# Reordering the start of a gated attention and mixture-of-experts layer: weight loads on two queues, a weight product in split parts, statistics of six tiles first

## Time and profile before

| | |
|---|---|
| median of 3 runs | 493.73 us |
| the profiled execution | 495.23 us |
| its span, first to last instruction | 493.5 us |
| TensorE busy (2146 matmul records) | 477.6 us, 97% |
| VectorE, ScalarE, GpSimd busy | 64%, 42%, 42% |
| mean rate of the 16 DMA engines | 235 GB/s |
| granted clock of TensorE | 1.00 in every slice |

### The profile page before, as it was taken

One profiled execution on the slowest core, in us unless ns is written; L12 is line 12 of the kernel. 1 busy time (PEld: TensorE's weight loads), 2 busy tenths in 40 slices (PEclk: granted clock), 3 DMA queues, 4 the chain that ended last, 5 costly groups with the idle time before them and its releaser, 6 DMA issues.

```text
span 493.5 us, 7143 instructions
## 1 busy us (share of the span) xinstructions
PE 477.6 (97%) x2146; PEld 388.1 (79%) x2147; DVE 315.2 (64%) x474; ACT 207.7 (42%) x300; POOL 205.3 (42%) x288
## 2 busy tenths in 40 slices
PE   3999999999999999999999999999999999999995
PEld 1678696888888878877888888888888878888884
DVE  2656253479553435969888888863597754857762
ACT  1156274132531144836444444322665441544550
POOL 3035301003887849802100000645657874377134
PEclk9999999999999999999999999999999999999999
DMA  7862999965889699896899566888455864445512
GB/s 253 313 242 107 379 383 362 394 239 185 301 267 308 233 317 289 256 293 202 245 279 229 191 184 205 277 308 304 129 156 166 277 182 155 146 147 181 170 43 86
DMA packets 77694, 115.77 MB, mean 235 GB/s; under 512 B 6608, under 2 KB 36320, under 8 KB 77664
## 3 DMA queue, kind: packets, MB, share of 16 engines
q1 hardware_dynamic: 64448, 78.66, 50.6%
q0 software_dynamic: 7360, 25.19, 14.6%
q10 hardware_dynamic: 5856, 11.54, 6.8%
HBM read 66.09 MB, written 49.28 MB: 234 GB/s over the span
## 4 chain that ended last, share of the span: by engine, by line
PE 70%; POOL 10%; DVE 6%; DMA 6%; issue 5%; ACT 1%; SPq 1%; DVEq 0%; ACTq 0%; POOLq 0%
PE ab L1583 17%; PE ab L1584 17%; PE ab L1585 17%; POOL rows_scratch L759 6%; PE sc L1583 4%; PE sc L1585 4%; PE sc L1584 4%; PE sc L1599 3%; POOL W L748 3%; DMA xg<-rows_scratch 2%; PE tp L1633 2%; PE tp L1589 2%; DMA rows_scratch<-xb,pos 2%; DMA raw_o<-in_w_out_t 1%; DVE y L1462 1%
## 5 line engine op out<-in xcount | busy, mean ns | idle before, releaser
L776 POOL DMA_INDIRECT y<-y_scratch,pos x32 | 33.4, 1043 | 88.7 <-DMA y_scratch<-yt_so 74.1
L1583 PE MATMUL ab<-W,st_h 128*128 x156 | 60.8, 390 | 1.1 <-DVE st_l L1291 1.1
L1584 PE MATMUL ab<-W,st_h 128*128 x156 | 60.7, 389 | 0.0
L1585 PE MATMUL ab<-W,st_l 128*128 x156 | 60.7, 389 | 0.0
L759 POOL DMA_INDIRECT rows_scratch<-xb,pos x32 | 31.2, 976 | 50.9 <-DVEq L1279 42.7
L1583 PE MATMUL sc<-xt_h,t_h 128*128 128x512 f32 x128 | 50.1, 391 | 0.0
L1585 PE MATMUL sc<-xt_h,t_l 128*128 128x512 f32 x128 | 49.8, 389 | 0.0
L1584 PE MATMUL sc<-xt_l,t_h 128*128 128x512 f32 x128 | 49.8, 389 | 0.0
L1020 ACT CAST st_h<-tp 128x512 fp32r<-128x512 f32 x39 | 22.9, 587 | 41.1 <-PE ab L1585 40.2
L1583 PEld LDWEIGHTS ab<-W,st_h 128*128 128x128 f32 x156 | 29.3, 188 | 7.6 <-issue 1.5
L1347 DVE TENSOR_REDUCE small<-sc 128x1 f32<-128x1024 f32 x16 | 19.5, 1222 | 23.7 <-PE sc L1585 23.4
(11 more groups left out here) (269 smaller groups left out, 1199.1 us busy)
## 6 DMA issues: line engine op xcount, KB each, us to landing
rows_scratch<-xn ACTq DMA_DIRECT2D x3, 3328.0 KB, 19.3
xb<-in_expert_w POOLq DMA_DIRECT2D x6, 1024.0 KB, 9.1
xn<-rows_scratch SPq DMA_DIRECT2D x48, 128.0 KB, 3.4
xg<-rows_scratch SPq DMA_DIRECT2D x44, 128.0 KB, 3.0
y_scratch<-yt_own SPq DMA_DIRECT2D x20, 256.0 KB, 3.2
y_scratch<-yt_so SPq DMA_DIRECT2D x19, 256.0 KB, 2.9
p_scratch<-prob SPq DMA_DIRECT2D x9, 512.0 KB, 2.7
rows_scratch<-xs SPq DMA_DIRECT2D x16, 256.0 KB, 5.9
```

The lines of the kernel that those rows point to most:

```text
L776: pool.indirect_dma_start(y[:, q, :], None, y_d, bass.IndirectOffsetOnAxis(pos[:, GB * s + p:GB * s + p + 1], 0))\
L1583: nc.tensor.matmul(dst, lh, rh, start=start, stop=False)
L1584: nc.tensor.matmul(dst, lh, rl, start=False, stop=False)
L1585: return nc.tensor.matmul(dst, ll, rh, start=False, stop=stop)
```

## The change

The loads of the output weights move to ScalarE's queue. The SP queue loads value weights and x in another order, then the bias columns, then (behind a wait on `vecs`) the second batch of x, and only then does it come to the row stores. The load of `b_out` moves from ScalarE's queue to GpSimd's, which issues it and the router's loads once the third pair of x tiles is in. Quarters 1 to 3 of the product for `nw` go through `product`, for which ScalarE makes high parts (`vr_h`, `or_h`), GpSimd one kind of low part (`vr_l`) and VectorE the other (`or_l`). The value bias is multiplied into the four quarters of the output weights by ScalarE, added up by GpSimd, and summed over the partitions by a single float32 matmul behind `values(0, 0)`. VectorE makes the statistics of six tiles before `first_stats`. Those of tiles 6 and 7 follow later, with their inverse root on GpSimd.

```diff
@@ SP queue
-            for c in range(KC):
-                sp.dma_start(raw[2][:, c, :], wqkv_v[2][:, c, :]).then_inc(vo_in[c], 16)
-                sp.dma_start(raw[3][:, c, :], wout_v[:, c, :]).then_inc(vo_in[c], 16)
+            def load_x(c):
                 w = slice(2 * c, 2 * c + 2)
                 sp.dma_start(xb[:, w, :], x_v[0][:, w, :]).then_inc(x_in[c], 16)
+            for c in range(KC):
+                if c == KC - 1:
+                    load_x(c - 1)
+                sp.dma_start(raw[2][:, c, :], wqkv_v[2][:, c, :]).then_inc(vo_in[c], 16)
+                if 1 <= c < KC - 1:
+                    load_x(c - 1)
+            sp.dma_start(bcols[:, :, :], b_qkv).then_inc(vec_in, 16)
+            load_x(KC - 1)
             for n in (0, 1):
                 sp.dma_start(raw[n][:, :, :], wqkv_v[n]).then_inc(qk_in[n], 16)
+            sp.wait_ge(vecs, 1)
+            for h in range(2):
+                w = slice(h * GB // 2, (h + 1) * GB // 2)
+                sp.dma_start(xb1[:, w, :], x_v[1][:, w, :]).then_inc(x1_in, 16)
...
@@ GpSimd
+            for c in range(1, KC):
+                pool.wait_ge(vo_hi, 2 * c - 1)
+                pool.tensor_tensor(vr_l[:, c, :], raw[2][:, c, :], vr_h[:, c, :], ALU.subtract).then_inc(vr_lo, 1)
+            pool.wait_ge(x_in[KC - 2], 16)
             pool.dma_start(rw[:, :, 0:E], router_w.rearrange("(p c) e -> p c e", p=P)).then_inc(rw_in, 16)
...
-            pool.wait_ge(vecs, 1)
-            for h in range(2):
-                w = slice(h * GB // 2, (h + 1) * GB // 2)
-                pool.dma_start(xb1[:, w, :], x_v[1][:, w, :]).then_inc(x1_in[h], 16)
+            pool.dma_start(bo_bc, b_out.rearrange("(a n) -> a n", a=1).to_broadcast([P, D])).then_inc(rw_in, 16)
+            pool.wait_ge(vo_hi, 2 * (KC - 1) + KC)
+            link(pool.tensor_tensor(bias_sum, bias_sum, raw[3][:, 1, :], ALU.add))
+            link(pool.tensor_tensor(raw[3][:, 2, :], raw[3][:, 2, :], raw[3][:, 3, :], ALU.add))
+            pool.tensor_tensor(bias_sum, bias_sum, raw[3][:, 2, :], ALU.add).then_inc(pre, 1)
+            pool.wait_ge(st1_done, 1)
+            batch_stats(pool, link, slice(FIRST, GB))
...
@@ ScalarE
-            act.dma_start(bcols[:, :, :], b_qkv).then_inc(vec_in, 16)
-            act.dma_start(bo_bc, b_out.rearrange("(a n) -> a n", a=1).to_broadcast([P, D])).then_inc(vec_in, 16)
+            for c in range(KC):
+                act.dma_start(raw[3][:, c, :], wout_v[:, c, :]).then_inc(vo_in[c], 16)
...
+            for c in range(1, KC):
+                act.wait_ge(vo_in[c], 32)
+                nc.scalar.copy(vr_h[:, c, :], raw[2][:, c, :]).then_inc(vo_hi, 1)
+                nc.scalar.copy(or_h[:, c, :], raw[3][:, c, :]).then_inc(vo_hi, 1)
+            act.wait_ge(vec_in, 16)
+            act.wait_ge(or_lo, KC - 1)
+            for c in range(KC):
+                nc.scalar.mul(bias_sum if c == 0 else raw[3][:, c, :], raw[3][:, c, :], bcols[:, 2, c:c + 1]).then_inc(vo_hi, 1)
...
             for t in range(GB):
+                if t + 2 == FIRST:
+                    act.wait_ge(ln_done, 2)
                 if t + 2 < GB:
                     normalise(t + 2)
...
@@ VectorE
+            def output_low(c):
+                dve.wait_ge(vo_hi, 2 * c)
+                vec.tensor_tensor(or_l[:, c, :], raw[3][:, c, :], or_h[:, c, :], ALU.subtract).then_inc(or_lo, 1)
...
-            for t in range(GB):
-                if t % 2 == 0:
-                    dve.wait_ge(x_in[t // 2], 16)
-                last = row_stats(0, t)
+            output_low(1)
+            for c in range(FIRST // 2):
+                dve.wait_ge(x_in[c], 16)
+                row_stats(0, 2 * c)
+                last = row_stats(0, 2 * c + 1)
+                if c in (0, FIRST // 2 - 1):
+                    output_low(2 if c == 0 else 3)
...
+            fold_low(1)
             lo(0)
-            for n in range(1, KC):
+            for n in range(2, KC):
                 fold_low(n)
-            fold_value_bias()
+            split_bias()
             for t in range(GB):
                 if t + 1 < GB:
                     lo(t + 1)
+                if t == 0:
+                    dve.wait_ge(x_in[FIRST // 2], 16)
+                    for k in range(FIRST, GB):
+                        last = row_stats(0, k)
+                    last.then_inc(st1_done, 1)
                 v_lo(0, t)
+                if t == 1:
+                    fold_value_bias()
@@ TensorE
             for c in range(KC):
-                pe.wait_ge(vo_in[c], 32)
+                if c:
+                    pe.wait_ge(or_lo, c)
+                    pe.wait_ge(vr_lo, c)
+                else:
+                    pe.wait_ge(vo_in[c], 32)
                 for n in range(KC):
-                    last = nc.tensor.matmul(sc[:, n // 2, n % 2, :], every_fourth(raw[2][:, c, :], n), raw[3][:, c, :],
-                                            start=(c == 0), stop=(c == KC - 1))
+                    dst = sc[:, n // 2, n % 2, :]
+                    if c == 0:
+                        nc.tensor.matmul(dst, every_fourth(raw[2][:, c, :], n), raw[3][:, c, :], start=True, stop=False)
+                    else:
+                        last = product(dst, every_fourth(vr_h[:, c, :], n), every_fourth(vr_l[:, c, :], n),
+                                       or_h[:, c, :], or_l[:, c, :], False, c == KC - 1)
...
-            bias_of_values(0)
-            bias_of_values(1)
             turn(0)
-            bias_of_values(2)
-            bias_of_values(3).then_inc(vecs, 1)
             for t in range(GB):
                 if t + 1 < GB:
                     turn(t + 1)
                 pe.wait_ge(lo_done, t + 1)
-                if t == 1:
-                    pe.wait_ge(pre_done, 1)
                 values(0, t)
+                if t == 0:
+                    bias_of_values()
```

More of the change, by code:

```diff
@@ L197, in gated_attention_moe @@
         quarters = tuple(xs[:, 2 * n:2 * n + 2, :].rearrange("p a n -> p (a n)") for n in range(2))
+        vr_h, vr_l = (v[:, 0:KC, :] for v in (v_h, v_l))
+        or_h, or_l = (v[:, KC:2 * KC, :] for v in (v_h, v_l))
         with ExitStack() as a:
@@ L247, in gated_attention_moe @@
         mw1_rows = mw1[:, :, :, :].rearrange("p a c n -> p (a c) n").bitcast(F32)
-        bvb = prob[:, 0:KC * P].rearrange("p (c n) -> p c n", c=KC)
+        bias_sum = prob[:, 0:D]
         bo_bc = so[:, 0, :]
@@ L275, in gated_attention_moe @@
         x_in = sems("x_in", KC)
-        x1_in = sems("x1_in", 2)
+        x1_in = sem("x1_in")
         ln_done = sem("ln_done")
         q_hi = sem("q_hi")
-        bc_done = sem("bc_done")
+        vo_hi = sem("vo_hi")
+        or_lo = sem("or_lo")
+        vr_lo = sem("vr_lo")
         const = sem("const")
@@ L446, in rsqrt, with batch_stats @@
                 link(eng.tensor_tensor(r, r, t, ALU.mult))
-        def batch_stats(eng, link, b):
-            w = slice(GB * b, GB * (b + 1))
+        def batch_stats(eng, link, w):
             me, mo = stats[:, w, 1], stats[:, w, 4]
@@ L465, in batch_stats @@
             eng.tensor_scalar(shift[:, w], a, -1.0, None, ALU.mult).then_inc(ln_done, 1)
+        FIRST = 6
         def first_stats(vec, link):
-            w = slice(0, GB)
+            w = slice(0, FIRST)
             me, mo = stats[:, w, 1], stats[:, w, 4]
@@ L735, in _ @@
                 pool.tensor_tensor(low[:, c, :], raw[m // 2][:, c, :], high[:, c, :], ALU.subtract).then_inc(qk_split, 1)
-            pool.wait_ge(st1_done, 1)
-            batch_stats(pool, link, 1)
+            pool.wait_ge(st1_done, 2)
+            batch_stats(pool, link, slice(GB, G))
             pool.wait_ge(xn_ready, G)
@@ L912, in _ @@
                     clear_slots(t - GB + 3)
-            act.wait_ge(ln_done, 2)
+            act.wait_ge(ln_done, 3)
             for g in range(GB, GB + 4):
@@ L1143, in _, with split_bias @@
             dve.sem_inc(ab_read, 2)
[L1145 to L1151, removed]
+            def split_bias():
+                dve.wait_ge(vec_in, 16)
+                vec.tensor_tensor(prod, bcols[:, 0, :], bcols[:, 1, :], ALU.mult).then_inc(pre, 1)
+                link(vec.tensor_copy(bc_hl[:, :, :, 0], bcols[:, 0:2, :]))
+                vec.tensor_tensor(bc_hl[:, :, :, 1], bcols[:, 0:2, :], bc_hl[:, :, :, 0], ALU.subtract).then_inc(pre, 1)
+            def output_low(c):
+                dve.wait_ge(vo_hi, 2 * c)
+                vec.tensor_tensor(or_l[:, c, :], raw[3][:, c, :], or_h[:, c, :], ALU.subtract).then_inc(or_lo, 1)
             def row_stats(b, t):
@@ L1195, in fold_value_bias @@
             def fold_value_bias():
+                dve.wait_ge(rw_in, 48)
                 dve.wait_ge(vecs, 1)
-                vec.tensor_tensor(sbias[:, :], ab[:, 1, :], bo_bc, ALU.add).then_inc(pre_done, 1)
+                vec.tensor_tensor(sbias[:, :], sc[:, 1, 1, :], bo_bc, ALU.add).then_inc(pre_done, 1)
             def fold_biases():
-                dve.wait_ge(rw_in, 32)
```

(32 more changed lines are left out.)

## The result

| | before | after |
|---|---|---|
| median | 493.64 us (4 runs, 493.2 to 494.23) | 502.21 us (4 runs, 500.71 to 503.37) |
| profiled execution, its span | 495.23, 493.5 | 500.71, 499.0 |
| tile 8's transposes begin | 60.42 us | 66.25 us |
| from there to the end of the span | 433.1 us | 432.7 us |

The ratio is 1.0165, interval 1.0139 to 1.019: slower by 8 us, where I had forecast 2.4 us faster. The last line of the table says where to look. What the profiled execution lost, 5.5 us of span, was lost before tile 8, and the stages behind it did move along as a block. These 5.5 us aren't the whole loss: the profiled execution of the kernel before was 1.6 us above its median, and that of the changed kernel was its fastest, with a mean granted clock of 0.993. The other three had 0.984 to 0.992 and took 502.15 to 503.37 us. No trace shows where they lost the rest.

A forecast was written before the change was run, and what follows sets the result against it. TensorE, busy 97% of the span, was taken as the bound. Values start 6.5 us earlier, 5.7 gained before the store wait gives back 3.3; 2.4 off the median 493.73 makes 491.3 us, range 489.3 to 493.5.

The forecast's parts named there:

- Loads: Kernel start: with b_out gone from there, first weights land and the first matmul starts at 4.9 us instead of 7.8.
- The product: Weight product on TensorE: 14.0 us in place of 15.92, ending at 18.9 against 23.8.
- Up to values(0, 0): Stretch before the first values: VectorE's chain sets their start, at 21.4 us against 27.91, 6.5 earlier.
- The new wait: SP queue: tile 0's store lands behind second-batch loads at 33.1 us, delaying normalise(4); gives back 3.3 of 5.7 us.
- rival 3: At normalise(4): the wait outlasts all gains if b_out is still in flight at 26 us; 497.7 us, chance 0.06.
- break-even: Tile 0's store landing at 35.5 us, 2.36 MB taking over 9.1 us, beyond which the kernel gets slower.
- Rival 4: TensorE idle about 31.4 to 34.0 us returns at the lower clock, losing up to 2.04 us: 493.3; chance 0.06.
- The sum from 58.0: Start of tile 8's transposes, forecast at 58.0 us instead of 60.42, with everything behind moving along.
- The split parts: Weight product: 12 float32 matmuls become three float32r matmuls each, 0.71 us per product instead of 0.86.

The follow-up runs named there:

- row stores first: Changed kernel, but SP stores tiles 0 to 3 before it waits for vecs and loads the second batch: 493.26 us, ratio 0.9972.
- additions late: Changed kernel, but GpSimd waits for ln_done before its three additions: 497.14 us, ratio 1.0051.
- both edits: Changed kernel with stores of tiles 0 to 3 before the vecs wait and GpSimd's additions after ln_done: 490.01 us, 0.9905; again 489.19 us, 0.9882.

## Why the prediction was wrong, by its own steps

**Loads: right. The product: right by luck.** I took 4.9 for the first matmul; it came at 4.32. The last part of the weight product starts at 19.19; I had its end at 18.9. So the product takes 15.1 us and not 14.0, and the earlier start hides it. Its first quarter took 10.52 - 4.32 = 6.2 us where I had 5.5: the cold start cost 2.8 us and not the 2.04 of the kernel before. `b_out` was the cause, as rows 4 had suggested, and the gain from it (3 us) is real.

**Up to values(0, 0): the step that failed first.** I put 21.4 and it was 24.72, since every VectorE duration there was a row of a time in which GpSimd stood still. I had asked of GpSimd's three additions only whether they are ready in time (they were, 22.3 said and 23.1 measured). I didn't ask whom they stop. They cost VectorE 1.1 + 0.8 + 0.35 = 2.3 us in three steps, on the path. About another 1 us came from the first step of the inverse root at 16.2 instead of 15.1. VectorE works without a pause from 11.56 to there, behind the third value quarter's landing at 10.36, and its low parts of the output weights take 1.1 to 1.4 us in place of my 0.69, each of the three beside a subtraction on GpSimd. With the same low parts, but that quarter landed at 9.4 and 9.3, the root starts at 15.3 and 15.2 (row stores first, additions late). So this us belongs to both, and no run parts them.

**The new wait: right in place and kind, too small in size.** I had the store of tile 0 land 7.9 us after `vecs`; it took 40.33 - 29.93 = 10.4. The second batch's second load, issued at 30.37, took 9.2 us to land, where I had 5.4 to 7.8 for both together; the store landed 0.7 behind it. Two terms were missing from the sum. The queue in the window 30.9 to 40.25 us:

```profile
q1 hardware_dynamic: 1502, 2.93, 92.2%
```

I had counted 2.36 MB up to the landing, the two loads and the one store. When it landed, 2.93 MB had moved, parts of the stores of tiles 1 to 3 among them, which SP had issued behind it by 33 us. These 0.57 MB are 1.5 us at 0.39 MB/us, an estimate. And the rate in the first 1.3 us was low (20 to 184 GB/s from 30.9 to 32.2): 0.09 MB moved where 0.51 would have at 0.39 MB/us, another 1.1 us. Why it is low stays open, no run tried it; GpSimd's loads before show 16 to 164 GB/s from 29.25 to 30.5 too. So the wait gave back more than all gains, which is the outcome of rival 3 but not its condition: `b_out`, issued at 17.24, had landed 4.1 us later. Its break-even was a landing at 35.5. I gave it 0.06 since I looked for the danger in `b_out` alone, and didn't see that a late `vecs` moves the landing one for one. Removing the wait moved the ratio by 0.0193 in the changed kernel and by 0.0146 (1.0051 to 0.9905) in the version with late additions, 7 to 9.5 us.

**Rival 4 happened too, twice.** I gave the lower clock 0.06 and only behind the gap of the store. It also came behind the pause of 2.5 us ahead of the first transposes, which the slow VectorE steps had made. That the pause must be that long is not shown: with both edits the clock fell once behind pauses of at most 0.6 us. From values(0, 0) to `vecs` it took 29.93 - 24.72 = 5.2 us instead of 3.8, and values(0, 3) 46.29 - 42.39 = 3.9 instead of 2.8.

The sum from 58.0 to 66.25: 3.3 (start of the values) + 1.4 (clock) + 2.5 (store) + 1.1 (clock) = 8.3, against 8.25. That explains the profiled execution. The forecast of 491.3 was missed by 10.9 us, and the 2.7 beyond this sum stay open: the profiled executions lie on opposite sides of the two medians, and no trace shows the slower executions of the changed kernel. The rivals were priced one at a time, each from a start at 21.4, but they feed each other: a slow step makes a pause, the clock falls behind it, both delay `vecs`, and the loads behind `vecs` hold the stores.

**The split parts: sized rightly, worth nothing.** The 1.8 us were TensorE's saving by the rows; the product ends some 1 to 2 us earlier with split parts (19.4 against 20.3 and 21.3). But I myself had VectorE's chain set the start, and taking the split work off VectorE and ScalarE gives the same time back: 489.58 and 489.54 us without split parts, 490.01 and 489.19 with them.

## What to carry to other kernels

Before a load is put ahead of other transfers of one queue, list who waits for those behind it, and count the wait from the latest moment at which the load may be issued, with what stands behind the store in the queue counted in. A piece of work given to GpSimd has a second price, the steps of VectorE beside it that read two SBUF operands, or normalise as L1200 does; read it off the columns: a step on six elements that lasts as long as GpSimd's instruction is that. And a small vector spread to 128 partitions doesn't belong at the head of the queues.

## What was unexpected of the hardware

- A VectorE addition of 128x6 took 1.27 us beside a GpSimd addition of 1.27 us, 0.17 without it. Instructions that read PSUM kept their 0.68.
- A spread of `b_out` (0.26 MB) over 128 partitions at the start lowered what all queues moved from 3 to 6 us from 1.09 to 0.72 MB in one pair of kernels and from 0.97 to 0.55 MB in the other, and cost 3.3 and 3.0 us. Issued behind the third pair of x tiles, it is on none of the chains shown.
- A store of 256 KB behind two loads of 1 MB in one queue took 9.3 us from issue to landing, against 2.0 us in the median of before.
- TensorE's clock fell to the lower level after pauses of 2.5 and 4.8 us, and in one profile of the version with both edits after pauses of at most 0.6 us with transposes between them, in the other profile of it not. The executions of the changed kernel had a mean granted clock of 0.984 to 0.993 and spread over 2.7 us.
